# Four chained layers on one core: the constants of two attention masks added on VectorE in PSUM instead of on GpSimd, mask bytes broadcast early, and no barrier ahead of the work

## The reference

```python
# layer 0: 16 heads of width 16; queries from the tokens, keys and values from context and tokens
attn = einsum("bkhd,bnhd->bhkn", q, kmat) / 16
attn = where(full_mask, attn, -inf); attn = softmax(attn)     # full_mask: mask0, then ones
out  = rmsnorm(attn @ v @ out_w + out_b + residual)           # then an MLP with gelu, + residual
# layer 1: layer norm, token shift, five mixed projections, a decaying state scanned over 64 tokens:
#   out_l = r_l . (faaaa * a_l + s);  s = a_l + w_l * s,  a_l = k_l (x) v_l   (32 heads of width 8)
#   then a group norm, a gate, Wo, and a second gated block (fWk, fWr, fWv)
# layer 2: self attention, cross attention, MLP, each behind a layer norm
scores = einsum("bhqd,bhkd->bhqk", q, k) / 4
scores = scores * mask - 10000.0 * (1.0 - mask)               # the two attentions of this change
probs  = softmax(scores)
# layer 3: attention on the layer-normed context with a boolean mask, out * tanh(gate) + x
```

## Time and profile before

| | us |
|---|---|
| median of three runs | 1041.89 |
| lowest and highest run | 1038.15, 1042.33 |
| the profiled execution | 1040.13 |
| its span, first to last instruction | 1038.2 |
| PE busy | 954.2 (92% of the span) |
| DVE busy | 745.7 (72%) |
| ACT busy | 587.8 (57%) |
| POOL busy | 540.6 (52%) |

### The profile page before, as it was taken

One profiled execution on the slowest core, in us unless ns is written; L12 is line 12 of the kernel. 1 busy time (PEld: TensorE's weight loads), 2 busy tenths in 40 slices (PEclk: granted clock), 3 DMA queues, 4 the chain that ended last, 5 costly groups with the idle time before them and its releaser, 6 DMA issues.

```text
span 1038.2 us, 27531 instructions
## 1 busy us (share of the span) xinstructions
PE 954.2 (92%) x10944; PEld 760.8 (73%) x10944; DVE 745.7 (72%) x1607; ACT 587.8 (57%) x1334; POOL 540.6 (52%) x666
## 2 busy tenths in 40 slices
PE   6868999898799999999999999999998879999996
PEld 4657877676478787778778777777775758887885
DVE  1378358878889979844765578779589979876764
ACT  2379753235355556578867672546653347655772
POOL 1365355535568856433465474256565655765331
PEclk9979999999899999999999999999999989999999
DMA  9601200100000110100011100000010000000001
GB/s 351 248 3 33 55 1 1 29 1 1 1 1 3 33 33 1 55 22 1 20 34 29 33 2 25 5 22 3 2 29 13 2 2 2 13 2 14 13 2 42
DMA packets 27501, 30.70 MB, mean 30 GB/s; under 512 B 14640, under 2 KB 24176, under 8 KB 26736
## 3 DMA queue, kind: packets, MB, share of 16 engines
q1 hardware_dynamic: 26352, 27.11, 8.0%
q10 hardware_dynamic: 1024, 1.85, 0.5%
HBM read 26.85 MB, written 2.10 MB: 28 GB/s over the span
## 4 chain that ended last, share of the span: by engine, by line
PE 53%; DVE 20%; DVEq 9%; issue 6%; POOL 5%; ACT 4%; POOLq 1%; DMA 1%; ACTq 0%
PE bank L494 7%; PE bank L506 7%; PE bank L399 7%; PE bank L378 6%; PE bank L366 6%; PE bank L391 4%; DVE lane L1007 3%; DVEq L1010 3%; DVE bank L1003 2%; PE bank L457 2%; PE bank L481 2%; PE bank L535 2%; DVEq L1004 2%; PE bank L524 2%; DVEq L863 2%
## 5 line engine op out<-in xcount | busy, mean ns | idle before, releaser
L1413 POOL TENSOR_TENSOR lane<-lane 128x512 f32<-128x512 f32 x160 | 167.3, 1052 | 183.4 <-DVE lane L884 103.6
L1180 ACT COPY lane<-bank 128x512 f32<-128x512 f32 x232 | 132.2, 592 | 149.2 <-PE bank L366 83.7
L366 PE MATMUL bank<-ident,lane 128*128 128x128 f32 x896 | 133.3, 283 | 20.2 <-POOL lane L1413 4.8
L366 PEld LDWEIGHTS bank<-ident,lane 128*128 128x128 f32 x896 | 103.2, 144 | 49.3 <-issue 22.2
L1482 POOL TENSOR_TENSOR lane<-lane 128x512 f32<-128x512 f32 x64 | 81.3, 1271 | 74.1 <-DVE lane L1007 73.4
L1007 DVE TENSOR_TENSOR_SCAN lane<-lane,bank 128x256 f32<-128x256 f32 x128 | 81.0, 674 | 5.0 <-issue 0.4
L882 DVE TENSOR_REDUCE lane<-lane 128x8 f32<-128x512 f32 x96 | 64.8, 675 | 18.0 <-ACT lane L1199 16.8
L1162 ACT ACTIVATE lane<-bank,vecs 128x256 f32<-128x256 f32 x112 | 55.6, 554 | 39.0 <-PE bank L366 38.8
L1199 ACT ACTIVATE lane<-lane 128x512 f32<-128x512 f32 x96 | 60.7, 636 | 23.0 <-DVE lane L864 22.6
L1148 ACT ACTIVATE lane<-lane 128x256 f32<-128x256 f32 x96 | 52.4, 595 | 28.9 <-POOL lane L1398 28.7
L494 PE MATMUL bank<-lane,w_d 128*128 128x256 f32 x256 | 60.8, 387 | 2.6 <-ACT lane L1162 1.1
(11 more groups left out here) (162 smaller groups left out, 2233.3 us busy)
## 6 DMA issues: line engine op xcount, KB each, us to landing
lane<-in_inT SPq DMA_DIRECT2D x16, 256.0 KB, 4.6
lane<-in_x SPq DMA_DIRECT2D x16, 256.0 KB, 2.8
w_d<-in_w_d SPq DMA_DIRECT2D x1, 3072.0 KB, 21.2
w_am<-in_w_am SPq DMA_DIRECT2D x1, 2048.0 KB, 15.1
lane<-in_inT SPq DMA_DIRECT2D x16, 128.0 KB, 3.0
lane<-in_ctx SPq DMA_DIRECT2D x8, 256.0 KB, 2.9
out_x<-lane SPq DMA_DIRECT2D x8, 256.0 KB, 2.2
w_c<-in_w_c SPq DMA_DIRECT2D x1, 1792.0 KB, 12.0
```

Of the source, the lines that this page charges most:

```text
L366: ins = pe.transpose(t[:, i * P:(i + 1) * P], src, ident[:, :])
L1180: s.copy(out, src).then_inc(bk.free_sem(key), 1)
L1413: p.tensor_tensor(q, q, den.unsqueeze(2).to_broadcast([P, n, 512 // n]), ALU.mult).then_inc(sig["normal"].sem, 1)
```

## The change

- Self and cross attention: both steps of the mask are done by DVE in place in the bank of the scores: a multiply, a drain, an add of the constant, a drain (L884 and L886 of the changed kernel). The maximum is then read from PSUM and written to a small tile in SBUF, and the last add reads PSUM. POOL's 64 adds and the signals `masked` and `added` are gone.
- Layer 0's mask bytes come by one broadcast DMA to all 128 partitions for each group (128 KB in place of 4 KB), and for the first four groups they are issued behind `w_am` and ahead of `w_b`; POOL's zeroing of their tiles is gone, and it no longer waits for PE before its first steps in the first four groups.
- No common barrier: DVE and ACT wait for the vectors and for DVE's and POOL's first few instructions only. The constant of the self mask and the tanh of the gate are computed in the first group's stage b, and their users wait for `ready` there. PE no longer waits for vectors and identity ahead of its first matmul, but at each lane's first transposes.
- `ORDER` and `BANKS` are written anew for all engines.

```diff
 ORDER = {
     "PE": (
-        "P0111110000222223333031211010120011021221021101021011002203021012321130210111332111112330100000000001233130211"
+        "P0111112010002202233333120111010021022121021011021011022003021022111021000000000000211211011110233021000002000"
...
     "SP": (
-        "0123PP0123PP110022331023001122000011110222213323333301232013"
+        "0123P0123PPP110022331023000000110221111331222233332301321302"
     ),
...
             def probsT(u):
+                if g < NL and u == 0:
+                    pe.wait_ge(load["vecs"].sem, load["vecs"].at(0))
...
         def _(pe):
-            pe.wait_ge(load["vecs"].sem, load["vecs"].at(0))
             emit("PE", streams(pe, nothing(), pe_a, pe_b, pe_c, pe_d))
...
                 if tag == "self":
-                    ins = v.tensor_tensor(grid(A.probs[j]), grid(t[:, :]), self_m[:, :].unsqueeze(1).to_broadcast([P, n, S]), ALU.mult)
+                    if g < NL:
+                        v.wait_ge(load["consts"].sem, load["consts"].at(0))
+                        v.wait_ge(ready.sem, ready.at(0))
+                    x = grid(t[:, :])
+                    by, plus = (m[:, :].unsqueeze(1).to_broadcast([P, n, S]) for m in (self_m, self_c))
                 else:
-                    ins = v.tensor_tensor(A.probs[j].rearrange("p (n k) -> p n k", n=4), t[:, :].rearrange("p (n k) -> p n k", n=4),
-                                          flat(L.cross_m).unsqueeze(1).to_broadcast([P, 4, P]), ALU.mult)
-                ins.then_inc(sig["masked"].sem, 1)
+                    if j == 0:
+                        v.wait_ge(sig["masks"].sem, sig["masks"].at(g, 2))
+                    x = t[:, :].rearrange("p (n k) -> p n k", n=4)
+                    by, plus = (flat(m).unsqueeze(1).to_broadcast([P, 4, P]) for m in (L.cross_m, L.cross_c))
+                v.tensor_tensor(x, x, by, ALU.mult)
+                v.drain()
+                v.tensor_tensor(x, x, plus, ALU.add)
+                v.drain()
...
-                j = step - 1
-                if 0 <= j < PT_ and tag != "l3":
-                    v.wait_ge(sig["added"].sem, sig["added"].at(g, PART[tag] + j + 1))
-                    shift(j, grid(A.probs[j]), bk.tile((g, tag, "scores", j))[:, 0:n])
+                    shift(j, grid(bk.tile((g, tag, "scores", j))[:, :]), A.nmax[:, j, :])
                     yield
...
+            if g == 0:
+                v.wait_ge(load["consts"].sem, load["consts"].at(0))
+                v.tensor_scalar(self_c[:, :], self_m[:, :], 10000.0, -10000.0, ALU.mult, ALU.add).then_inc(ready.sem, 1)
...
             v.wait_ge(load["vecs"].sem, load["vecs"].at(0))
-            v.wait_ge(load["consts"].sem, load["consts"].at(0))
...
-            v.wait_ge(ready.sem, ready.at(0))
+            v.wait_ge(ready.sem, ready.at(0, 2))
...
-            for step in range(PT_ + 2):
-                if step < PT_ and tag != "l3":
-                    p.wait_ge(sig["masked"].sem, sig["masked"].at(g, PART[tag] + step + 1))
...
-                    p.tensor_tensor(q, q, c, ALU.add).then_inc(sig["added"].sem, 1)
-                    yield
...
+            for j in range(PT_):
+                p_normal(p, g, tag, j, A.probs[j], A.den[:, j, :], 2 * PT_)
+                yield
...
-                for j in range(4):
-                    sp.dma_start(L.mask0_raw[32 * j:32 * j + 1, :], a["mask0"][g]).then_inc(sig["mask0_loaded"].sem, 16)
+                sp.dma_start(L.mask0_raw, a["mask0"][g].partition_broadcast(P)).then_inc(sig["mask0_loaded"].sem, 16)
```

More of the change, by code:

```diff
@@ L887, in v_attention @@
                 j = step
-                if step < PT_ and tag != "l3":
-                    masked(j)
-                    yield
-                if step < PT_ and tag == "l3":
-                    key = (g, tag, "scores", j)
-                    v.wait_ge(bk.full_sem(key), bk.full_at(key))
-                    if j == 2:
-                        v.wait_ge(bk.full_sem((g, tag, "scores", PT_ - 1)), bk.full_at((g, tag, "scores", PT_ - 1)))
-                    shift(j, grid(bk.tile(key)[:, :]), A.nmax[:, j, :])
-                    yield
-                j = step - 1
-                if 0 <= j < PT_ and tag != "l3":
-                    v.wait_ge(sig["added"].sem, sig["added"].at(g, PART[tag] + j + 1))
-                    shift(j, grid(A.probs[j]), bk.tile((g, tag, "scores", j))[:, 0:n])
+                if step < PT_:
+                    if tag != "l3":
+                        masked(j)
+                        yield
+                    else:
+                        key = (g, tag, "scores", j)
+                        v.wait_ge(bk.full_sem(key), bk.full_at(key))
+                        if j == 2:
+                            v.wait_ge(bk.full_sem((g, tag, "scores", PT_ - 1)), bk.full_at((g, tag, "scores", PT_ - 1)))
+                    shift(j, grid(bk.tile((g, tag, "scores", j))[:, :]), A.nmax[:, j, :])
                     yield
@@ L1270, in s_b @@
             s.activation(L.lora[0:32, 1, :], t[0:32, T:2 * T], ACT.Tanh).then_inc(bk.free_sem(key), 1)
+            if g == 0:
+                s.wait_ge(load["consts"].sem, load["consts"].at(0))
+                s.activation(tgate[:, 1:2], tgate[:, 0:1], ACT.Tanh).then_inc(ready.sem, 1)
             yield
@@ L1376, in _ @@
             s.wait_ge(load["vecs"].sem, load["vecs"].at(0))
[L1377 to L1379 removed]
+            s.wait_ge(ready.sem, ready.at(0, 2))
             emit("ACT", streams(s, nothing(), s_a, s_b, s_c, s_d))
@@ L1529, in _ @@
             p.memset(ones_bf[:, :], 1.0)
-            for lane_ in lanes:
-                p.memset(lane_.mask0_raw, 0)
             p.drain().then_inc(ready.sem, 1)
-            p.wait_ge(ready.sem, ready.at(0))
             emit("POOL", streams(p, nothing(), p_a, p_b, p_c, p_d))
```

101 lines of the change are left out of this document (43 added, 58 removed).

## The result

The changed kernel takes 1052.76 us (median of 4 runs, 1051.6 to 1058.47) beside 1041.16 for the kernel before on the same chip. The ratio is 1.0134, 95% interval 1.0107 to 1.0162: slower by some 1.3%. The forecast was 1058, slower, and the time lies in its range. The profiled execution took 1052.57 us with a span of 1050.5, which is 12.3 more than before.

A forecast was written before the change was run, and what follows sets the result against it. PE was taken as the bound by busy share (954.2 of 1038.2 us), but DVE as full from 185 to 411 and 776 to 863 us. From 1040.1 us, -11 - 4 + 43 - 10 = +18 gave 1058 us, range 1048 to 1072.

The forecast's parts named there:

- The start, -11: Up to 100 us: first scores at about 23.5 us instead of 43.34, PE idle time 11 us less.
- 10 or more was the sign set for it: Check on the start: PE idle from 0 to 100 us by 10 us or more less.
- The clock, -4: From 40 to 100 us: half of the 9.7 us lost to PE's lower clock comes back, 4 us.
- DVE and POOL: Busy time in the changed profile: DVE 790 us, POOL 459; L884 and L886 at 0.69 us each, 0.75 or more start to start.
- The full stretches, +43: Two stretches where state scans meet attention: counting both engines' lists, PE's forced idle time goes from 30 to 73 us.
- both signs set for it (32 and 41): Check on the full stretches: PE idle 32 us or more in the first half's, 41 or more in the second's.
- the 50 under which the forecast would have given up the +43 and its sign: Check: PE idle under 50 us in the two full stretches together means the +43 fails, and with it the sign.
- rival 1: DVE's new work falls into its idle time and the kernel gets faster, 1027 us; chance 0.19.
- Its split, 27 from the new work and 16 from the order: Of the +43, 29 tiles x 0.93 = 27 us is new mask work; 16 is the order laying more scans beside attention.
- DVE's time between 411 and 776 us costs nothing: From 411 to 776 us PE is the bound and DVE has 115 us to spare, so added DVE time is free.
- What comes back, -10: DVE no longer waits 5.3 us for POOL and POOL's chain to PE is less crowded: together 10 us less.
- The fixed part of PSUM reads: 64 maxima reading PSUM instead of SBUF: forecast 0; by the skill's rule 4 us more.

The follow-up runs named there:

- e5_one_op: The changed kernel with one VectorE minimum with a constant tile per mask tile in place of multiply and add: 1045.15 us, ratio 1.0061.
- e6_one_op_old_order: The kernel before, its order, barrier and loads kept, with one in-place VectorE minimum per mask tile for DVE's multiply and POOL's add: 1038.01 us, ratio 0.9995.

## Why the prediction was right, and where it was not

**The start, -11.** The scores stood at 24.15 as said (23.5, and up to 2 us for the masks). The forecast had the mask ready at 22; it overlooked that POOL makes the first lane's mask before the second's, which the first scores need (23.50). Idle time fell by 6.6 and not 11 (10 or more was the sign set for it). The term was too large: of the 16.1 us between 40 and 100 only 6 were to stay, and 10.2 did. The term's causes were right, as the start alone gave 1.3 us and the rest needs the new list.

**The clock, -4.** From 40 to 100 us the granted clock is 1.00 for 0.89, so this came back. It was lost again in the two stretches, at 0.93 and 0.92 where PE stood still more often. Over the span PE's busy time is 2.1 us less.

**DVE and POOL.** Busy 785.5 and 460.3, predicted 790 and 459. The added instruction was sized well, 0.70 us, and 0.77 from start to start.

**The full stretches, +43.** DVE needed 152.4 us twice, as counted, at a busy share of 90%. But PE's idle time there rose by 25.8 us and not 43, and both signs set for it (32 and 41) were missed: 21.7 and 29.8. A part of what the count called idle went into slower matmuls: PE was busy 253.3 us there for a listed 236.3, before 167.5 for 159.1, 8.6 us more. That makes 34 of 43. This is the term that was mis-sized. Idle and slower matmuls together, the count was nearer than the split of before and after suggests: 34.1 for a counted 30 before, 68.5 for 73 after. The idle time of 51.5 us was only just over the 50 under which the forecast would have given up the +43 and its sign, and under which rival 1 was to win.

**Its split, 27 from the new work and 16 from the order, was the wrong step.** The two can't be told apart by adding them. In the old order the added instructions cost 48 us, in the new one 7.6, and the new order with one instruction costs 10 over the old. The new list leaves DVE waits, and a second instruction per tile takes the place of 37 us of them; a third finds 3 and costs 47. By the traces of `e5_one_op` and the changed kernel, the two stretches hold 10 us of delay for the forecast's 27. The prediction's premise that DVE's time between 411 and 776 us costs nothing is refuted: in the old order the two attentions at 515 to 577 us cost 8.5 us of delay (18.4 to 26.9). The stretches were too long to show why: DVE is full inside each attention, for 10 to 20 us at a time, and the mean over 365 us hides it.

**What comes back, -10.** Idle time outside start and stretches fell by 4.8 us. The hop to POOL can be sized from `e6_one_op_old_order`: without the hop and with a drained minimum in place (64 x 0.16 = 10 us more on DVE's list) it is equal to the kernel before, so the hop is worth about what those drains cost where they count, at most 10 us. No run sizes it by itself.

**The fixed part of PSUM reads.** The rule of the Trainium skill (VectorE: DVE Perf Modes, section The TRN2 errata) gives, as an estimate from its figures, 4 us more for 64 maxima from PSUM. The trace does not agree: 683 ns for 96 maxima from PSUM, 681 for those from SBUF that wrote to PSUM, and 674 for 96 sums with both ends in SBUF.

**The sum.** The start gave less than forecast, the stretches cost less, and the errors offset each other: +12.3 for +18. The sign came from the stretches, as forecast. Rival 1 had held that the new work falls into idle time and the kernel gets faster; its first half nearly holds, since only 7.6 of 49 us are paid in the new order, but the place for them was bought with a list that is 10 us slower with one instruction per tile. Against the forecast's terms the start missed by +4.4 us, what comes back by +5.2, PE's busy time by +1.9 and the idle time of the stretches by -17.2. That these add up to only -5.7 is in part luck.

## What to carry to other kernels

When in-order engines pass work around, don't price an added instruction by the busy share of its engine over a long stretch. Ask in the timeline whether the engine waits inside the few microseconds of work into which the instruction goes. Here DVE was busy 76 to 84% over stretches of 17 to 27 us and waited hardly at all inside the attention; each added instruction cost its whole 0.77 us, 4 tiles x 16 attentions, until the order was written anew and left waits to fill. An order fits the instruction count and the sequence that it was written with: changing either under it cost 20 to 48 us, and a second instruction in the order made for it 7.6. So test an instruction's worth with the order held and with the order made for it. And look for a form that needs fewer instructions: the minimum with a constant tile took POOL's adds away at no cost in the old order (0.9995), and with the early start it was the fastest kernel here (0.9969).

## What was not expected of the hardware

Two drained instructions of 128x512 elements in PSUM follow each other at 0.76 to 0.77 us where each is busy 0.69 to 0.70. So an engine that goes through its list with hardly a gap showed a busy share of 90% (137.6 and 138.1 of 152.4 us).

The granted clock fell in stretches where PE paused (0.83 from 582 to 602 us, 0.91 from 600 to 640, 0.92 and 0.93 in the two full stretches, all above), and the matmuls left took longer there: by the count of the list 8.6 us more in the two stretches of the changed kernel than before, beside 25.8 of idle time.
